# A graph network's edge stage: tile 194's source rows fetched by ScalarE, three rows in each of 44 steps

## What is computed

```python
# layer 0
edge_input = concat([x[src], edge_attr_32])
messages = gelu(edge_input @ mW1 + mb1) @ mW2 + mb2
gates = sigmoid(gelu(edge_input @ gW1 + gb1) @ gW2 + gb2)
aggregated = segment_sum(messages * gates, dst)
h = x + (gelu(concat([x, aggregated]) @ uW1 + ub1) @ uW2 + ub2)
x1 = layernorm(x + layernorm(h) * ln_g + ln_b)
# layer 1
score = exp(clip(heads(K[src] * Q[dst] * E / sqrt(12)), -5, 5))
x = layernorm(x1 + segment_sum(V[src] * score, dst) / (segment_sum(score, dst) + 1e-6))
```

## Time and profile before

| | |
|---|---|
| median of 3 runs | 1237.32 us (1236.41 to 1237.65) |
| the profiled execution | 1236.37 us, its span 1234.6 us, mean TensorE clock 0.942 |
| POOL | busy 931.4 us (75%), 975 indirect DMAs, the same share in every slice |
| PE | busy 987.1 us (80%) |
| DVE | busy 946.1 us (77%) |
| ACT | busy 688.0 us (56%) |
| edge stage / update stage / attend stage on PE | about 15 to 271 / 273 to 700 / 751 to 1158 us |

### The profile page before, as it was taken

One profiled execution on the slowest core, in us unless ns is written; L12 is line 12 of the kernel. 1 busy time (PEld: TensorE's weight loads), 2 busy tenths in 40 slices (PEclk: granted clock), 3 DMA queues, 4 the chain that ended last, 5 costly groups with the idle time before them and its releaser, 6 DMA issues. The chain is left out here.

```text
span 1234.6 us, 25653 instructions
## 1 busy us (share of the span) xinstructions
PE 987.1 (80%) x5213; PEld 627.4 (51%) x5213; DVE 946.1 (77%) x4242; ACT 688.0 (56%) x1522; POOL 931.4 (75%) x979
## 2 busy tenths in 40 slices
PE   5999999989999999999999505878887888888300
PEld 2555555548878878787877402433333333333100
DVE  3544444446999999999999963999999999999700
ACT  2555544432678788787878663555555555555300
POOL 6777777777777777777777777777777777777777
PEclk9999999999999999999999757999999999999755
DMA  7888888653567667677777445555555444434100
GB/s 170 235 231 229 226 227 217 139 156 108 187 210 229 212 222 225 213 226 217 229 209 232 143 159 131 146 143 133 132 144 140 128 128 135 133 115 131 37 31 30
DMA packets 174571, 206.35 MB, mean 167 GB/s; under 512 B 105195, under 2 KB 119596, under 8 KB 174505
## 3 DMA queue, kind: packets, MB, share of 16 engines
q1 hardware_dynamic: 140565, 159.21, 41.6%
q0 software_dynamic: 31200, 45.93, 15.9%
q10 hardware_dynamic: 2740, 0.60, 0.3%
HBM read 101.23 MB, written 77.58 MB: 145 GB/s over the span
## 5 line engine op out<-in xcount | busy, mean ns | idle before, releaser
L476 POOL DMA_INDIRECT out<-rows,put_at x196 | 190.6, 972 | 59.7 <-issue 35.0
L435 POOL DMA_INDIRECT agg_d<-rows,put_at x196 | 189.6, 967 | 59.8 <-issue 52.1
L426 POOL DMA_INDIRECT rows<-in_x,src_i x195 | 184.3, 945 | 62.1 <-issue 59.1
L454 POOL DMA_INDIRECT rows<-agg_d,dst_at x194 | 183.5, 946 | 60.5 <-issue 53.5
L469 POOL DMA_INDIRECT node_work<-agg_d,src_i x194 | 183.1, 944 | 59.1 <-issue 56.7
L719 ACT ACTIVATE node_work<-node_work,nshift,nscale 128x96 f32<-128x96 f32 x392 | 145.7, 453 | 81.8 <-DVE nshift L976 81.7
L754 ACT ACTIVATE rows<-yc,cshift,cscale 128x96 f32 (+1 forms) x196 | 75.5, 456 | 98.4 <-DVE cshift L1096 98.4
L853 DVE SCALAR_TENSOR_TENSOR ps<-hidden,ps 96x512 f32<-96x512 f32 x49 | 33.9, 691 | 125.5 <-ACT hidden L698 125.5
L487 PE MATMUL ps<-ident,x_in 128*96 128x128 f32 x588 | 81.7, 275 | 53.9 <-DMA ea<-in_edge_attr 52.7
L578 PE MATMUL ps<-uW2s,nT 97*128 97x96 f32 x784 | 99.7, 281 | 16.6 <-ACT nT L739 15.9
L940 DVE BATCH_NORM_STATS2 bn<-ps 128x6 f32<-128x96 f32 x392 | 100.2, 260 | 16.3 <-PE ps L578 16.1
(11 more groups left out here) (150 smaller groups left out, 2150.8 us busy)
## 6 DMA issues: line engine op xcount, KB each, us to landing
agg_d<-zeros SPq DMA_DIRECT2D x40, 480.0 KB
x_in<-in_x SPq DMA_DIRECT2D x49, 384.0 KB
node_work<-agg_d SPq DMA_DIRECT2D x49, 384.0 KB
agg_d<-node_work SPq DMA_DIRECT2D x49, 384.0 KB, 3.0
out<-node_work SPq DMA_DIRECT2D x49, 384.0 KB
mask<-cont_d SPq DMA_DIRECT2D x49, 208.0 KB
ein<-rows SPq DMA_DIRECT2D x49, 192.0 KB
mask<-cont_d SPq DMA_DIRECT2D x49, 192.0 KB
```

The costliest lines, as they stand in the source:

```text
L426: pool.indirect_dma_start(rows[:, g * EJ + j, :], None, x, rows_at(src_i, g, j)).then_inc(xs_gathered[g % 2][j], 16)
L435: pool.indirect_dma_start(agg_d, rows_at(put_at, g, j), rows[:, g * EJ + j, :], None).then_inc(agg_added[g % 2][j], 16)
L454: pool.indirect_dma_start(rows[:, g * EJ + j, :], None, x1_d, rows_at(dst_at, g, j)).then_inc(xd_gathered[g % 3][j], 16)
L476: pool.indirect_dma_start(out, rows_at(put_at, g, j), rows[:, g * EJ + j, :], None, bounds_check=N - 1, oob_is_err=False).then_inc(out_sca ...
```

## The change

POOL's first pass loses its last gather, tile 194. ACT instead fetches that tile's 128 rows: it loads the tile's 128 indices into `tail_a` at the start (four more entries are zeros), and in each of the loop's 44 steps, after the tanh, it loads three of them into registers and copies the three rows of x, from HBM to HBM, into `tail_a_d`. In its step for the last group SP waits for all 132 copies, copies 128 rows of `tail_a_d` to tile 194 of `rows`, waits for that copy, and loads the group as before. One more memset raises the counts that wait on pads_set.

```diff
+AFIRST, ASTEPS = 3, 44
+        tail_a_d = nc.dram_tensor("tail_a_d", [ASTEPS * 3, D], F32).ap()
+        tail_a = sb("tail_a", [1, ASTEPS * 3], I32)
...
             def edge_step(i, q, inner, zeroing=False):
...
                     if last:
-                        sp.wait_ge(tail_x_placed, 16)
-                    for j in range(EJ - 1 if last else EJ):
+                        sp.wait_ge(tail_a_fetched, 16 * ASTEPS * 3)
+                        sp.dma_start(rows[:, TFULL - 1, :], tail_a_d[0:P, :]).then_inc(tail_x_placed, 16)
+                        sp.wait_ge(tail_x_placed, 32)
+                    for j in range(EJ - 2 if last else EJ):
                         sp.wait_ge(xs_gathered[s][j], per_slot(i + 2, s))
...
-                for j in range(EJ - 1 if g == EFULL else EJ):
+                for j in range(EJ - 2 if g == EFULL else EJ):
...
-            act.wait_ge(pads_set, 7)
+            act.wait_ge(pads_set, 8)
...
+            act.wait_ge(pads_set, 8)
+            act.dma_start(tail_a[0:1, 0:P], src[TFULL * P - P:TFULL * P].rearrange("(a p) -> a p", a=1)).then_inc(tail_a_loaded, 16)
             act.wait_ge(edge_weights_loaded, EDGE_WEIGHTS)
+            act.wait_ge(tail_a_loaded, 16)
...
                     act.activation(gate[:, :], ps[0:D, 5, :], ACT.Tanh, bias=gb2s[:, 0:1], scale=0.5).then_inc(tanh_done, 1)
+                if inner:
+                    k = i * 3 - AFIRST * 3
+                    _, nodes = nc.values_load_multi_w_load_instructions(tail_a[0:1, bass.DynSlice(k, 3)], engines=[mybir.EngineType.Activation], min_val=0, max_val=N - 1,
+                                                                        skip_runtime_bounds_check_because="src holds rows of x")
+                    for n, node in enumerate(nodes):
+                        act.dma_start(tail_a_d[bass.DynSlice(k + n, 1), :], x[bass.DynSlice(node, 1), :]).then_inc(tail_a_fetched, 16)
...
+            dve.memset(tail_a[:, P:], 0).then_inc(pads_set, 1)
```

More of the change, by code:

```diff
@@ L236, in build @@
         lnb_placed = sem("lnb_placed")
+        tail_a_loaded, tail_a_fetched = sem("tail_a_loaded"), sem("tail_a_fetched")
         tail_x_loaded, tail_x_fetched, tail_x_placed = sem("tail_x_loaded"), sem("tail_x_fetched"), sem("tail_x_placed")
@@ L275, in _ @@
             sp.dma_start(next_r[:, 0, :], dst[1:TQ * P + 1].rearrange("(q p) -> q p", p=P)).then_inc(index_loaded, 16)
-            sp.wait_ge(pads_set, 4)
+            sp.wait_ge(pads_set, 5)
             tile_load(src_r, src, 0, src_loaded)
@@ L828, in _ @@
             dve.tensor_scalar(need[:], pairs[:], 16, None, ALU.mult).then_inc(needs_made, 1)
-            dve.wait_ge(pads_set, 7)
+            dve.wait_ge(pads_set, 8)
             dve.wait_ge(edge_weights_loaded, EDGE_WEIGHTS)
```

## The result

The changed kernel takes 1295.5 us (median of 5, 1294.64 to 1297.63) against 1237.32 us: ratio 1.0471, interval 1.046 to 1.0482, 58 us slower. The forecast was 1307, with 1255 to 1338 as the range.

A forecast was written before the change was run, and what follows sets the result against it. Two chains bound the kernel: POOL's DMA count, and edge stage to update stage to last x1 store, later by 0.56 us. Period 61 + stage end 9 - POOL 0 = 70 us on the span, giving 1307 us; range 1255 to 1338.

The forecast's parts named there:

- The joint: POOL's third pass, group 47: edge-stage delay reaches the kernel's end one for one; the gain on POOL alone gives 0.
- Rival D: Update stage starts no later or its DVE stream has room, last x1 store stays at 729: 1237 us; chance 0.04.
- ScalarE's covered part: Edge stage: issuing starts just after the tanh begins, window 1.7 us; the period stays 5.055 us up to 2.1 us.
- rival C: No run-ahead (issues begin only after the tanh ends), or waits for SP's issues: 1334 or 1335 us; chance 0.14.
- T: ScalarE's issue time per edge step: 1.05 us before the first copy, 0.65 and 2 x (0.65 + 0.25), 3.5 us.
- rival B: Cheap issue on ScalarE, copies nearer SP's 0.24 us, 2.0 to 2.8 us per step: 1245 to 1276 us; chance 0.18.
- The queue's own work: ScalarE's loop in the edge stage: about 0.25 us per step besides instructions and issuing.
- the period: Edge step, tanh to tanh: 6.47 us instead of 5.055, 1.41 longer over 43 intervals, 61 us.
- The end: Edge stage's end: SP's wait, copy and load of group 48 move PE's turn from 2.38 to 11.5, 9.1 us more.
- The lock: Descriptor block held by one sequencer, ScalarE's issues wait for SP's: 43 x 0.65 = 28 us, 1335; chance 0.05.
- Rival E: Edge stage: idle time drops TensorE from 2.4 to 1.2 GHz, 44 x 5 us more, 1450 us; chance 0.04.
- The zero stores: Stores of agg_d paced by edge steps, some 49 us later; POOL's second pass 16 us late, covered.

## Why the prediction was right

**The joint.** That a delay of the edge stage goes through to the end one for one, and a gain on POOL alone doesn't, was the base of the argument. It held: in 13 of the study's 14 traces the last x1 store follows PE's first matmul of the update stage at 455.5 to 458.7 us, while that start moves from 272 to 401 us. Rival D falls with it. The other is the kernel before with 16 more gathers, with 461.0; there POOL's scatters, which the update stage reads, come 20 us later, and the store no longer sets the end.

**ScalarE's covered part.** The queue did start the load within 0.1 us of the tanh's start, as taken from rows 7; rival C falls. The free window of 2.1 us held: 1.6 us of issuing (one row) cost 1 us, 2.4 us cost 18.

**T.** Forecast 3.5, measured 1.04 + 2.08 = 3.1 us, above the 2.8 up to which rival B went. The mis-sized term is the issue: 0.527 us on ScalarE's queue, where SP's own needs 0.647 in the same form. The 1.05 us to the first issue was right as a sum, though the load in it took 0.71 and not 0.5; the 0.25 us between issues was right (0.245). The queue's own work was 0.33, not 0.25. Together the period came to 6.19, taken over two steps, in most of the loop and, with the long first ones, to 6.24 in the mean, instead of 6.47: 50 us instead of 61. On the span 61.2 us stand against 70; these 11 us too many are more than the whole difference, and the end of the stage gave 2 of them back.

**The end.** 9.1 us forecast, 7.2 measured: each landing took 1.8 to 1.9 us where rows 4 gave 2.3 to 3.0. The half clock, left in the range at 1 to 4 us, took 3.8 and should have stood in the sum, since some 8 us of idle time on PE were forecast (7.00 measured). With it the forecast would have been some 74 us and further off, so this omission is luck that hid a part of the period's 11 us.

**The lock.** SP's issues are as long beside ScalarE's as without them: the row copy 607/647/678 ns before, and

```profile
L325 SPq DMA_DIRECT2D tail_d<-in_x x40: 607/647/688, 15.4 to 251.1; - x40
```

after. The lock that the Trainium skill describes (Perfetto Trace Analysis, "DMA Instruction — HWDGE") has no price in these medians; single issues of up to 1.2 us are the exceptions in which it may show. The floor of about 600 ns that the Trainium skill gives for a register load (DMA: Bandwidth & Descriptors, "Latency and other measured facts") doesn't hold as a floor, 275 ns were seen, but it is nearer to ScalarE's medians than the 281 ns of SP that I preferred.

**The clock.** Rival E was put as a fall to half for the whole loop. In the full change it didn't happen (1.00). It does begin a little further on, in part: 0.92 to 0.98 with four rows, 0.81 to 0.88 with the issues into SBUF.

**POOL.** The zero stores held the second pass back by 8.5 us, not by 16, as the steps were stretched less than forecast; in the third pass POOL waited 114.6 - 59.1 = 55.5 us over its dispatch, as forecast.

## What to carry to other kernels

Issuing a DMA is work of the engine's queue, here 3.1 us in each step, and a compute engine shows it as idle time: before moving issues there, find the gap in its own loop, from the start of the last instruction ahead of it (the queue runs ahead) to the moment at which the next one's input is ready, and count loads, address arithmetic and issues against it. What fitted cost next to nothing here (1 us for one row), what didn't was paid in each step; the same issuing was nearly free in two gaps and cost 50 us in one. Where work is spread over many steps, let the last portion end well ahead of its user, since behind it stand a landing, a copy and a load in series. And look for the second chain before counting a gain on the busiest engine: here it lay 0.56 us away.

## What the runs showed of the hardware that I had not expected

- A register load from SBUF on ScalarE's queue takes from 0.28 to 1.56 us, with medians of 0.72, 0.78, 0.71 and 0.31 us for one, two, three and four values, and 1.02 for four at another stride, so the number of values doesn't order them. With four values the address does: 0.31 us at multiples of 16 bytes from the start of the tile, 0.90 to 1.35 us elsewhere. For fewer values the cause is open.
- The same row copy from HBM to HBM is issued in 0.527 us by ScalarE and 0.647 us by SP. A quarter of a row into SBUF at an address from a register takes ScalarE 0.757 us.
- Of a pause of 7.00 us on PE came 3.8 us of half clock, and even ones of 2.15 and 1.88 us were followed by matmuls of double length. Pauses of 1.1 to 1.4 us in each step left the clock at 1.00; with 1.4 and 1.7 us in turn it was 0.92 to 0.98.
